# Attention scores and probabilities kept for 64 keys per 32 queries, with the instruction orders laid out anew

## What is computed

```python
def shift_tokens(t):                       # half of the features come from the token before
    a, s = jnp.split(t, 2, -1)
    s = jnp.pad(s, ((0, 0), (1, 0), (0, 0)))[:, :-1]
    return jnp.concatenate([a, s], -1)

def local_attention(q, k, v):              # w = WINDOW = 32, n = 128
    bq = q.reshape(b, h, nw, w, d)         # four groups of 32 queries
    bk2, bv2 = look(bk), look(bv)          # each sees its own 32 keys and the 32 before: 64 keys
    mask = (it < jb) | (it > jb + w) | (jb == -1)
    sim = jnp.einsum('bhwie,bhwje->bhwij', bq, bk2) * QK_SCALE
    attn = jax.nn.softmax(jnp.where(mask, -jnp.finfo(sim.dtype).max, sim), -1)
    return jnp.einsum('bhwij,bhwje->bhwie', attn, bv2).reshape(b, h, n, d)

for i in range(6):
    x = attn_layer(shift_tokens(x), Wqkv[i], q_scale[i], k_scale[i], Wo[i]) + x
    x = ffn_layer(shift_tokens(x), ln_g[i], ln_b[i], W1[i], b1[i], W2[i], b2[i]) + x
```

## Time and profile before

| what | value |
|---|---|
| median of three runs | 1836.76 us |
| the profiled execution | 1836.35 us |
| its span, first to last instruction | 1834.6 us |
| PE busy | 1702.5 us, 93% |
| DVE busy | 1604.0 us, 87% |
| POOL busy | 1533.9 us, 84% |
| ACT busy | 1416.7 us, 77% |
| TensorE clock granted over the span | 0.979 |

### The profile page before, as it was taken

How to read it: one execution, slowest core, us unless ns; L and a number is a source line. 1 busy time by engine, 2 the same in 40 slices (tenths; PEclk the granted TensorE clock), 3 DMA queues, 4 the chain that set the end, 5 groups by cost and what they waited for, 6 DMA issues and landing times.

```text
span 1834.6 us, 39770 instructions
## 1 busy us (share of the span) xinstructions
PE 1702.5 (93%) x14065; PEld 1372.6 (75%) x14256; DVE 1604.0 (87%) x2852; ACT 1416.7 (77%) x4889; POOL 1533.9 (84%) x2056
## 2 busy tenths in 40 slices
PE   6589999999999999999999999999999999999995
PEld 4468777787787777787777877877777777778774
DVE  4588898998998989989989999989899899899982
ACT  3278878878788787787797787887877887978872
POOL 2489988898988988988989888889888889898870
PEclk9599999999999999999999999999999999999997
DMA  3000010000010000001000001000001000000000
GB/s 114 2 1 3 3 46 2 4 17 1 8 46 1 4 17 1 8 3 44 4 1 17 8 1 46 5 1 17 4 5 46 3 2 16 1 8 4 1 4 26
DMA packets 24154, 25.38 MB, mean 14 GB/s; under 512 B 13795, under 2 KB 21654, under 8 KB 23190
## 3 DMA queue, kind: packets, MB, share of 16 engines
q1 hardware_dynamic: 23958, 22.83, 4.1%
HBM read 18.65 MB, written 1.05 MB: 11 GB/s over the span
## 4 chain that ended last, share of the span: by engine, by line
PE 71%; DVE 19%; ACT 3%; issue 3%; POOL 3%; DMA 1%; SPq 0%; POOLq 0%; DVEq 0%
PE ps L410 9%; PE ps L382 8%; PE ps L402 7%; PE ps L369 7%; PE ps L390 7%; PE ps L362 7%; PE ps L364 5%; PE ps L363 5%; DVE xh L975 4%; PE ps L377 3%; PE ps L441 3%; DVE ss L905 2%; DVE t L920 2%; DVE t L922 2%; ACT pr L620 2%
## 5 line engine op out<-in xcount | busy, mean ns | idle before, releaser
L620 ACT ACTIVATE pr<-ps,nmax 128x128 f32<-128x128 f32 x1536 | 549.2, 389 | 28.2 <-DVE nmax L939 25.4
L743 POOL TENSOR_TENSOR t<-t 128x512 f32<-128x512 f32 x384 | 500.4, 1303 | 75.7 <-DVE t L922 75.7
L777 POOL TENSOR_TENSOR pr<-pr,rsum 128x512 f32<-128x512 f32 x384 | 406.5, 1059 | 22.8 <-DVE rsum L946 22.1
L765 POOL TENSOR_TENSOR t<-t,rn 128x512 f32<-128x512 f32 x384 | 402.5, 1048 | 21.8
L620 ACT ACTIVATION_READ_ACCUMULATOR pr<-ps,nmax 128x1 f32 x1536 | 352.4, 229 | 0.0
L585 ACT ACTIVATE sq<-ps 128x512 f32<-128x512 f32 x384 | 235.4, 613 | 116.0 <-PE ps L364 112.1
L920 DVE TENSOR_TENSOR t<-ps,rope 128x512 f32<-128x512 f32 x384 | 262.3, 683 | 42.0 <-ACT sq L585 37.5
L362 PE MATMUL ps<-w_hi,xt_hi 128*128 128x512 f32 x576 | 280.1, 486 | 14.3 <-DVE t L922 10.0
L369 PE MATMUL ps<-consts,t 128*128 128x128 f32 x1536 | 239.1, 278 | 29.4 <-ACT qT L612 26.1
L922 DVE TENSOR_TENSOR t<-ps,rope 128x512 f32<-128x512 f32 x384 | 260.5, 678 | 0.0
L905 DVE TENSOR_REDUCE ss<-sq 128x8 f32<-128x512 f32 x384 | 252.0, 677 | 3.6 <-ACT sq L585 2.6
(11 more groups left out here) (121 smaller groups left out, 2879.0 us busy)
## 6 DMA issues: line engine op xcount, KB each, us to landing
wqkv<-wqkv_in SPq DMA_DIRECT2D x6, 1536.0 KB, 12.3
wo<-wo_in SPq DMA_DIRECT2D x6, 512.0 KB, 9.6
xsh<-xr SPq DMA_DIRECT2D x24, 127.0 KB
w<-w_in SPq DMA_DIRECT2D x6, 342.0 KB, 7.5
w<-w_in SPq DMA_DIRECT2D x6, 172.5 KB
x<-x_in SPq DMA_DIRECT2D x4, 256.0 KB, 4.9
out<-x SPq DMA_DIRECT2D x4, 256.0 KB, 2.9
ctx<-ctx_in SPq DMA_DIRECT2D x4, 240.0 KB, 4.5
```

Of the source, the lines that this page charges most:

```text
L620: i = A(pr[:, g, k, :], ps[:, S_BANK[odd], k * P:(k + 1) * P], ACT.Exp, bias=nmax[:, h2, odd, k:k + 1], accum_out=psums[:, h2, odd, k:k + 1])
L743: G.tensor_tensor(t1[:, c, :], t1[:, c, :], t2[:, c, :], ALU.add).then_inc(qk_added[c], 1)
L765: G.tensor_tensor(w, w, rn[:, par(u), h2, a, :].unsqueeze(2).broadcast_to([P, 8, E]), ALU.mult).then_inc(done, 1)
L777: G.tensor_tensor(w, w, rsum[:, g // 2, g % 2, :].unsqueeze(2).broadcast_to([P, 4, P]), ALU.mult).then_inc(pr_ready[g], 1)
```

## The change

Scores. Four groups of 32 queries are formed, and each gets only a window of 64 keys that starts at key 0, 0, 32 or 64. A head is then four matmuls with 32 weight columns (the queries) and 64 moving columns (the keys), each on its own 32 PSUM partitions. Both banks now hold all 16 heads of a unit, in 64 columns each, so there is one mask write, one `row_max` and one wait per unit where there were two.

Probabilities. `exps` works on 128 x 64. An even head and the odd head beside it lie next to each other in `pr`, so one 128 x 128 transpose takes both: eight transposes per unit, two copies, two `normalise_p`. After it, the keys of even heads are on partitions 0 to 63 and those of odd heads on 64 to 127, at window positions. So v has to lie there too: four DMAs per unit (`shift_v`) copy 64 rows of v each into `v_win`. The host orders the columns of the v weights by even and odd heads, and the rows of Wo to match. `weigh_values` is 48 matmuls per unit with 64 rows and 64 weight columns, of 64 or 32 moving columns; they use all four quarters of the array.

Token shift. The DMA moves whole rows (127 rows of 512 elements) in place of half rows, and POOL then overwrites the first half, after the DMA and no longer beside it.

Orders. The lists of all engines are new; there are 109 steps, from -7 to 101. The inverse norms of a unit are made once for q and k of all heads. The copy of the transposed K0 moves from DVE to ACT. The weights of the next layer come in six DMAs, one per chunk. x is transposed for the next layer earlier against its use.

```diff
-    band = np.where((k <= q) & (q <= k + WIN), 0.0, MASKED)      # 128 keys
+SPAN = 64
+WINDOW_START = [0, 0, 32, 64]
+    k = np.array(WINDOW_START)[q // WIN] + np.arange(SPAN)[None, :]
...
 # PE
-            def scores(u, h2):
-                for odd in range(2):
-                    mm(ps[:, S_BANK[odd], :], ident16[:], band16[:].rearrange("p a k -> p (a k)"), start=True, stop=False,
-                for k in range(4):
-                    for odd in range(2):
-                        r = slice(E * odd, E * odd + E)
-                        i = mm(ps[:, S_BANK[odd], k * P:(k + 1) * P], qT[r, par(u), 4 * h2 + k, :], kT[r, par(u), 4 * h2 + k, :],
+            def scores(u):
+                for odd in range(2):
+                    mm(ps[:, S_BANK[odd], :], ident16[:], band16[:].rearrange("p c w -> p (c w)"), start=True, stop=False,
+                for c in range(BLOCKS):
+                    for g in range(P // WIN):
+                        for odd in range(2):
+                            r, q = slice(E * odd, E * odd + E), slice(WIN * g, WIN * g + WIN)
+                            i = mm(ps[q, S_BANK[odd], c * SPAN:(c + 1) * SPAN], qT[r, par(u), c, q],
+                                   kT[r, par(u), c, WINDOW_START[g]:WINDOW_START[g] + SPAN],
...
-            def transpose_p(u, g):
-                    i = tr(ps[:, TP_BANK[g], k * P:(k + 1) * P], pr[:, g, k, :], ident)
+            def transpose_p(u, h2):
+                    i = tr(ps[:, TP_BANK[h2], k * P:(k + 1) * P], pr[:, 4 * h2 + k, :], ident)
...
-            def weigh_values(u, h2):
-                for k in range(4):
-                    for odd in range(2):
-                        i = mm(ps[odd * E:odd * E + E, O_BANK[h2], k * P:(k + 1) * P], v[:, par(u), h * E:(h + 1) * E], pT[:, g, k, :],
+            def weigh_values(u):
+                even = [(0, 2 * WIN, v[0:E, p, 0]), (2 * WIN, WIN, v_win[0:E, p, 0]), (3 * WIN, WIN, v_win[0:E, p, 1])]
+                odds = [(0, 2 * WIN, v_win[E:P, p, 0]), (2 * WIN, WIN, v_win[E:P, p, 1]), (3 * WIN, WIN, v[E:P, p, 1])]
+                for j in range(BLOCKS // 2):
+                    for n in range(3):
+                        for b in range(2):
+                            for odd in range(2):
+                                c = 2 * j + b
+                                q, m, window = (even, odds)[odd][n]
+                                i = mm(ps[E * b:E * b + E, O_BANK[odd], j * P + q:j * P + q + m], window[:, c * E:(c + 1) * E],
+                                       pT[E * odd:E * odd + E, c, q:q + m], start=True, stop=True)
...
 # SP
+            def shift_v(u, odd):
+                sp.wait_ge(v_ready[odd], u + 1)
+                if u >= 2:
+                    sp.wait_ge(o_ps, 4 * (u - 1))
+                p, r = par(u), slice(E * odd, E * odd + E)
+                starts = WINDOW_START[1:3] if odd else WINDOW_START[2:4]
+                for n, t in enumerate(starts):
+                    sp.dma_start(v_win[r, p, n, :], v[t:t + SPAN, p, odd, :]).then_inc(v_shifted[odd][p], 16)
-                sp.dma_start(xsh[1:P, :, E:P], xr[0:P - 1, s, E:P]).then_inc(f_shifted, 16)
+                sp.dma_start(xsh[1:P, :, :], xr[0:P - 1, s, :]).then_inc(f_shifted, 16)
...
 # ACT
-                    i = A(pr[:, g, k, :], ps[:, S_BANK[odd], k * P:(k + 1) * P], ACT.Exp, bias=nmax[:, h2, odd, k:k + 1],
+                    i = A(pr[:, c, odd * SPAN:(odd + 1) * SPAN], ps[:, S_BANK[odd], c * SPAN:(c + 1) * SPAN], ACT.Exp,
...
 # POOL
-                pool.wait_ge(x_updated, f * QUAD + QUAD)
+                pool.wait_ge(f_shifted, 16 * (f + 1))
                 G.tensor_copy(xsh[:, :, 0:E], xr[:, s, 0:E]).then_inc(f_half, 1)
-            def refine_norm(u, h2):
+            def refine_norm(u):
-            def normalise_p(u, g):
+            def normalise_p(u, h2):
...
 # DVE
-            def row_max(u, h2):
-                dve.wait_ge(s_ps[h2], 2 * u + 2)
+            def row_max(u):
+                dve.wait_ge(s_ps, 8 * u + 8)
...
-    FIRST_STEP, LAST_STEP = -3, 107
+    FIRST_STEP, LAST_STEP = -7, 102
```

More of the change, by code:

```diff
@@ L38 @@
 Q0, K0, Q1, K1, V0, V1 = range(6)
-def head(g, k):
-    return 8 * (g // 2) + 2 * k + g % 2
+SPAN = 64
+WINDOW_START = [0, 0, 32, 64]
+BLOCKS = H // 2
 def constants():
@@ L198, in run_input, with run_layer @@
             task((s - lag) // QUAD + NQ)
-    def at(s, lag, l):
-        return s - lag == l * B
+    def run_layer(s, lag, task, first=0, last=L):
+        if (s - lag) % B == 0 and first <= (s - lag) // B < last:
+            task((s - lag) // B)
     def par(u):
@@ L229, in _, with load_qkv @@
                     sp.dma_start(x1[:, s, :], x_d[s].rearrange("b t d -> t b d")).then_inc(ld_x[q + 1], 16)
-            def load_qkv(l):
+            def load_qkv(l, c):
+                w = slice(CHUNK_COLS[c], CHUNK_COLS[c] + 512)
                 if l >= 1:
-                    for c in range(6):
-                        sp.wait_ge(w_ready[c], l)
-                sp.dma_start(wqkv[:], wqkv_d[l]).then_inc(ld_qkv, 16)
+                    sp.wait_ge(w_ready[c], l)
+                sp.dma_start(wqkv[:, w], wqkv_d[l, :, w]).then_inc(ld_qkv[c], 16)
             def load_scales(l):
@@ L264, in shift_tokens, with step @@
                     sp.wait_ge(const_ready, 9)
-                sp.dma_start(xsh[1:P, :, E:P], xr[0:P - 1, s, E:P]).then_inc(f_shifted, 16)
-            load_qkv(0)
+                sp.dma_start(xsh[1:P, :, :], xr[0:P - 1, s, :]).then_inc(f_shifted, 16)
[7 more added lines that the diff above has]
+                    sp.dma_start(v_win[r, p, n, :], v[t:t + SPAN, p, odd, :]).then_inc(v_shifted[odd][p], 16)
+            def step(s):
+                run_layer(s, -15, load_scales, 1)
+                run_layer(s, -4, load_w1, 1)
+                run_layer(s, 6, load_w2, 1)
+                run_layer(s, -11, lambda l: load_qkv(l, Q0), 1)
+                run_layer(s, -10, lambda l: load_qkv(l, K0), 1)
+                run_layer(s, -9, lambda l: load_qkv(l, Q1), 1)
+                run_layer(s, -8, lambda l: load_qkv(l, K1), 1)
+                run_layer(s, -7, lambda l: load_qkv(l, V0), 1)
+                run_layer(s, -6, lambda l: load_qkv(l, V1), 1)
+                run(s, 1, shift_v, 1)
+                run_quad(s, 6, shift_tokens)
+                run_layer(s, 2, load_wo, 1)
+                run(s, 0, shift_v, 0)
+            for c in range(6):
+                load_qkv(0, c)
             load_scales(0)
@@ L272, in _ @@
             sp.dma_start(vec[:], vec_d.rearrange("l p v -> p l v")).then_inc(ld_vec, 16)
[L273 to L286, removed]
+            for s in range(FIRST_STEP, LAST_STEP):
+                step(s)
             for q in range(NQ):
@@ L528, in step @@
[L528 to L530 removed]
+                    scores(s - 1)
             pe.wait_ge(ld_const, 80)
@@ L644, in step @@
             def step(s):
-                run(s, 2, exps, 2)
-                run(s, 0, square, K0)
-                run(s, 0, upper_w, K0)
-                run(s, 2, exps, 3)
-                run(s, 2, upper_w, V1)
                 run(s, 0, square, Q0)
```

513 lines of the change are left out of this document (250 added, 263 removed).

## The result

The changed kernel takes 1923.5 us (median of 4 runs, 1914.2 to 1925.9) against 1836.6 us before: the ratio is 1.046, with a 95% interval of 1.043 to 1.050. The forecast was 1613 us, faster, with a range of 1543 to 1790. It is wrong in sign and by 310 us. A slower outcome had 0.12, but none of the rivals names the cause.

What follows compares the result with a forecast made beforehand. PE was taken to bound the kernel, DVE close behind. PE work 13.93 us plus waits 0.9 and 0.7 made 15.53 a unit; 96 units, 1491, plus 120 gave span 1611, time 1613 us; range 1543 to 1790, the forecast's own 1543 to 1677.

Steps and rivals of the forecast that it cites:

- slower outcome: Changed kernel slower than before: chance 0.12, from half of the fixed price, two places and alone.
- the unit of 17.86 us: Kernel before: PE, busy 17.12 us of each unit, sets the end, with DVE close behind at 16.31.
- The transposes and the other engines: Per unit: eight of 16 PE transposes go, -0.88 us; DVE falls to 13.85, POOL to 12.80, ACT to 12.83.
- Scores and values side by side: PE's split-array blocks: all places run together; per unit scores take 1.61 us (saving 1.61), values 1.54 (saving 0.70).
- two places: Rival, chance 0.09: only two array places run side by side in scores and values; unit 18.4 us, 1888 us.
- fixed price: Rival, chance 0.04: each PE record costs the same whatever its size; at 25 ns 1831 us, no gain.
- alone: Rival, chance 0.01: each record of the new PE blocks runs by itself; PE 24.1 us a unit, over 2400 us.
- the sum: PE's work 13.93 us a unit plus waits 0.9 and 0.7: 15.53; new blocks' records counted at 2.22 us.
- 8 us on: hidden too: Whole-row token shift: issued in mid-step, DVE asks for it 8 us later, so its transfer costs nothing.
- not hidden at all: Upper case for the token shift: DVE stands 4.9 us once a quad, 1.2 us a unit.
- (a): PE waits for ACT's copy of Q1, 0.7 us, and for K0's copy, 0.2: 0.9 us a unit.
- (b): Once per quad DVE's first gated product waits for the values; DVE loses 2.7 us, 0.7 a unit.

Runs made afterwards that it cites:

- e1: The changed kernel with each token shift in two DMAs of 112 and 15 rows in place of one of 127: 1743.2 us, ratio 0.951.
- f0: TensorE alone on constant data, only matmuls of the kernel's shapes: 1280 score records back to back take 35.7 us, 960 value records 25.7 us.
- f3: e1 with the values block moved behind the next step's two v projections, v held three deep, ScalarE's values copy behind its exponentials: 1677.6 us, ratio 0.914.
- h1: f3 with the scores block in two halves of 64 records, the first behind the K0 projection: 1669.8 us, ratio 0.910.
- h2: f3 with the values block in two halves of 48 records around the V0 projection: 1688.9 us, ratio 0.921.
- f2: e1 with the first two groups of 32 queries in one product of 64, 96 score records in place of 128: 1868.8 us, ratio 1.019.
- g1: f2 with its score products sorted by width, all of 64 queries first and then all of 32: 1700.8 us, ratio 0.927.
- f1: e1 with the spans of v moved for the first two units only: 1752.5 us, ratio 0.955.

## Why the prediction was wrong

*What bounds the kernel before, the unit of 17.86 us:* right.

*The transposes and the other engines:* right; a unit's busy times came within 0.13 us on each of DVE, POOL and ACT.

*Scores and values side by side:* the mechanism is right, "two places", "fixed price" at 25 ns and "alone" are out. Sizes: the values' 1.54 us measured 1.53. The scores were to start 7 ns apart and start 10 ns apart, so the block with its masks takes some 0.3 us more than the 1.61 forecast. By the 25 ns between starts of the Trainium skill ("TensorE: Matmul & The Clock Gate", Part 1) the 128 records would take 3.2 us; the measurement, 1.41, decides for the sum.

*"8 us on: hidden too":* this step failed and turned the sign. The earlier trace rows gave 4.9 us for 256 KB in 128 rows from x_in; the shift moves 254 KB in 127 rows and took 13.9 to the copy. The error was to price a transfer by its bytes when its shape decides, and to leave the upper end at the price of another shape: with 13.9 us for 4.9, "not hidden at all" would have stood beside the rivals. Second, the wait was placed on DVE alone. In the quad above DVE asks 9.8 us after the issue and POOL already 5.2 us after it, and POOL's queue behind the copy (norms, products of q and k) took most of it. Cost: after minus e1, 18.88 - 16.96 = 1.92 us a unit, 180 us. Without it the time would have been 1743.2, inside the range to 1790 and beyond the forecast's own 1677.

*What the sum did not hold at all:* the supply of instructions. The prediction saw 224 records at 10 ns each and asked only whether the array could. In e1 the two blocks take 1.70 + 2.46 us against 1.41 + 1.53: 1.21 us a unit, 116 us. f0 shows it alone; f3 gives back 66 us, of which the blocks hold 51.

*The two waits (a) and (b):* both are there in e1. Over 76 units, DVE's gated product stands 0.74 us a unit (forecast 0.7), and PE's weight loads for the copies of Q1 and K0 about 0.66 (0.9):
```profile
DVE hT L1018 <- PE ps L471: 55.9, 20, 3.3
...
PEld ps L394 <- ACT qT L639: 31.2, 56, 0.9
...
PEld ps L421 <- ACT kT L639: 18.8, 46, 1.3
```
*Does the rest add up?* The unit less the excess of the two blocks is 16.96 - 1.21 = 15.75 in e1, 16.29 - 0.68 = 15.61 in f3, 16.23 - 0.43 - 0.17 (the halving) = 15.63 in h1; the forecast's was 15.53. So two causes outside the sum hold nearly all of the 310 us. This is arithmetic: no run here is without the stops, and of the 57 us between h1 and the forecast it is open how much could be had.

That 15.6 to 15.8 comes so near to 15.53 is partly luck. In e1, whose stretch from 200 to 1700 us holds 88.4 units, PE is busy for 1364.5 us, 15.43 a unit, where 13.93 were forecast, and stands for 1.53. Of the blocks' 1.21 some 0.90 are idle time (80.0 us of `issue` before L410 and L440) and 0.31 count as busy. That leaves 15.1 of work and 0.6 of standing against 13.93 and the 1.6 kept for two waits: too little work and too much waiting in the sum, by about as much. Two parts of the missing work have a name. One is the 0.3 of the scores above. The other is a reading: the trace of before lacks the records of the first masks, as the prediction says, so that PE's 17.12 us do not hold them, while the 1.61 us taken off do. PE stands idle in their place for 28.2 us in 84 units, 0.3 a unit:
```profile
L377 PE MATMUL ps<-band,ident 128*128 128x512 bf16 x168 | 63.6, 379 | 28.2 <-issue 22.5 <-ACT pr L620 2.6
```
The other half of the missing work was not taken apart. The granted clock, 0.94 in the changed kernel, follows PE's idle time: in e1 and f3, where PE idles less, it is 0.98 and 0.99.

## What to carry to other kernels

Price a transfer by its outermost count as well as its bytes: 127 rows went through one engine and took 13.9 us from issue to the copy, 112 and 15 landed in 2.5 and 2.3. When work on TensorE is cut into small pieces, count instructions per stretch, weight loads too: here 128 records arrive at best every 3.3 to 4.0 us, some 200 are in hand (f0), and a denser run stops whatever the array could do; put long products between the dense blocks, and count what each further way into and out of the split array costs (h1, h2). And when a helper is moved behind a transfer that it used to run beside, ask what its own queue holds, before asking who reads the data.

## What the hardware showed that I had not expected

- A run of 224 small records without a long product between them loses 1.5 us in the mean in e1 (61 units), and 0.3 where the FFN's products stand between (21 units). On average the kernel needs a record every 67 ns (28,560 in 1924 us), and f0 sustains one every 28: only the burst counts.
- Eight places of 64 rows by 32 columns take float32 records 10 ns apart, and go back to full-size work in 0.15 us; alternating 64 and 32 columns costs about 0.14 us each time (f2 against g1).
- Cutting the transfers from 46 to 15 GB/s gave nothing (f1): SBUF to SBUF moves of 64 rows, four of 128 KB a unit, are as good as free here.
